# One transpose for the oldest and the own key tile, and one for the global keys of four units, in a sliding-window attention and FFN layer

## The reference, cut to what matters

```python
# attention of one sequence: T = 2048 tokens, D = 2048, 16 heads of 128, G = 16 global tokens
xn = layernorm(x) * ln_scale + ln_bias
xg = concat([global_tokens, xn])
Q, K, V = xg @ Wq.T, xg @ Wk.T, xg @ Wv.T
band = (j <= i) & (j >= i - 256 + 1)          # plus: every token sees the 16 global keys
attn = softmax(Q @ K.T / sqrt(128) masked by band)
x = layernorm(x + (attn @ V) @ Wo.T + x)
# ffn, hidden size 5632, weights as integers 0..255
x = layernorm(x + down(silu(gate(x)) * up(x)))
```

## Time and profile before

| what | value |
|---|---|
| time, median of 3 runs | 3033.59 us (3030.71 to 3200.52) |
| the profiled execution's own time | 3030.48 us |
| its span, slowest core (core 1) | 3028.9 us; all cores 3017.3 to 3028.9 us |
| mean granted TensorE clock of the cores | 0.993 to 0.995 |
| PE busy | 2943.5 us, 97% of the span, 16928 matmuls |
| PE weight loads busy | 1517.8 us, 50% |
| DVE busy | 1112.9 us, 37% |
| ACT busy | 603.1 us, 20% |
| POOL busy | 213.3 us, 7% |
| chain that ended last | PE 95%, DVE 1%, DMA 1%, ACT 1%, issue 1% |

### The profile page before, as it was taken

How to read it: one execution, slowest core, us unless ns; L and a number is a source line. 1 busy time by engine, 2 the same in 40 slices (tenths; PEclk the granted TensorE clock), 3 DMA queues, 4 the chain that set the end, 5 groups by cost and what they waited for, 6 DMA issues and landing times.

```text
span 3028.9 us, 43253 instructions; the slowest of 8 cores (3017.3 to 3028.9 us)
## 1 busy us (share of the span) xinstructions
PE 2943.5 (97%) x16928; PEld 1517.8 (50%) x16928; DVE 1112.9 (37%) x2185; ACT 603.1 (20%) x1364; POOL 213.3 (7%) x349
## 2 busy tenths in 40 slices
PE   4899999999999999999999999999999999999998
PEld 2566666666665444444444444444444444444443
DVE  5645555555556564112121211111222333212224
ACT  4434444444444111000000000000111111100000
POOL 0000000000000000000000000010000000012220
PEclk9999999999999999999999999999999999999999
DMA  7132413223214563434343435565655555448442
GB/s 200 69 57 46 74 33 68 52 41 64 54 25 150 170 205 112 84 70 84 70 83 70 82 65 104 104 109 143 132 115 122 113 123 126 97 103 189 77 77 112
DMA packets 93944, 293.54 MB, mean 97 GB/s; under 512 B 9008, under 2 KB 33840, under 8 KB 82480
## 3 DMA queue, kind: packets, MB, share of 16 engines
q0 software_dynamic: 46224, 172.05, 33.5%
q1 hardware_dynamic: 46656, 118.02, 11.1%
q10 hardware_dynamic: 864, 0.70, 0.1%
HBM read 412.45 MB, written 50.33 MB: 153 GB/s over the span
## 4 chain that ended last, share of the span: by engine, by line
PE 95%; DVE 1%; DMA 1%; ACT 1%; issue 1%; POOL 0%; DVEq 0%; ACTq 0%; SPq 0%; POOLq 0%
PE pb L789 40%; PE pb L836 19%; PE pb L341 14%; PE pb L372 7%; PE pb L725 7%; PE pb L453 2%; PE pb L472 2%; PE pb L419 1%; ACT xnfmt L313 1%; DMA wdt<-wd 1%; DVE smt L272 1%; PE pb L394 0%; PE pb L707 0%; PE pb L302 0%; DMA xt<-x 0%
## 5 line engine op out<-in xcount | busy, mean ns | idle before, releaser
L789 PE MATMUL pb<-xn2t,wgt 128*128 128x512 bf16 x2816 | 636.5, 379 | 0.0
L789 PE MATMUL pb<-xn2t,wut 128*128 128x512 bf16 x2816 | 636.5, 379 | 0.0
L341 PE MATMUL pb<-xnfmt,wqkt 128*128 128x512 bf16 x2048 | 537.2, 382 | 10.5 <-ACT kgt L364 5.8
L803 DVE SCALAR_TENSOR_TENSOR hmidt<-pb,sutt,silt 128x512 bf16<-128x512 f32 x176 | 132.2, 751 | 908.0 <-PE pb L789 898.3
L836 PE MATMUL pb<-wdt,hmidt 128*128 128x512 bf16 x2048 | 446.8, 380 | 7.3 <-DVE wdt L686 6.1
L789 PEld LDWEIGHTS pb<-xn2t,wut 128*128 128x128 bf16 x2816 | 275.5, 98 | 332.3
L789 PEld LDWEIGHTS pb<-xn2t,wgt 128*128 128x128 bf16 x2816 | 275.6, 98 | 331.9
L799 ACT ACTIVATE silt<-pb,sgtt 128x512 f32<-128x512 f32 x176 | 119.9, 687 | 1288.8 <-PE pb L789 1288.7
L836 PEld LDWEIGHTS pb<-wdt,hmidt 128*128 128x128 bf16 x2048 | 200.8, 98 | 251.5 <-issue 12.0
L372 PE MATMUL pb<-wvt,xnfmt 128*128 128x256 bf16 x2048 | 269.0, 273 | 0.0
L341 PEld LDWEIGHTS pb<-xnfmt,wqkt 128*128 128x128 bf16 x2048 | 173.8, 98 | 142.0 <-issue 20.7
(11 more groups left out here) (73 smaller groups left out, 1867.0 us busy)
## 6 DMA issues: line engine op xcount, KB each, us to landing
wgt<-wg POOLq DMA_DIRECT2D x88, 512.0 KB, 5.2
wut<-wu POOLq DMA_DIRECT2D x88, 512.0 KB, 7.2
wdt<-wd POOLq DMA_DIRECT2D x64, 512.0 KB, 5.9
xt<-x SPq DMA_DIRECT2D x16, 1024.0 KB, 8.9
v1t<-x SPq DMA_DIRECT2D x16, 1024.0 KB, 5.4
r2sp<-v1t SPq DMA_DIRECT2D x16, 1024.0 KB, 3.9
wdx<-wd POOLq DMA_DIRECT2D x24, 512.0 KB, 5.7
wqkt<-wk POOLq DMA_DIRECT2D x16, 512.0 KB, 8.2
```

What stands on the lines that cost most here:

```text
L341: t1 = op("pe", lambda e, dc=dc: e.matmul(pb[bank][:, :], w[:, dc * 128:(dc + 1) * 128], xnfm[:, dc * T + b * 512:dc * T + (b + 1) * 512], ...
L789: ins = e.matmul(pb[bank][:, :], w[gu][:, dc * 128:(dc + 1) * 128], xn2[p][:, dc * 1024 + tc * 512:dc * 1024 + tc * 512 + 512], start=(dc ...
L803: bfree[bu] = sil_free[s] = op("dve", lambda e, bu=bu, s=s, hsl=hsl: e.scalar_tensor_tensor(hsl, pb[bu][:, :], sut[:, hb:hb + 1], silt[s][ ...
```

## The change

The scores are computed as before. Then, for a unit with t of at least 2, the own tile's scores are overwritten with the oldest tile's wherever the mask allows the oldest tile (a predicated copy, L465 in the new file), which leaves 272 columns in place of 400 for the maximum, the exp and the scaling. The scaling writes t-1 and the merged tile (256 columns) to `pnt` and the 16 global columns to `pgt`, at columns 32*(u%4), which collects four units. PE transposes the merged tile and t-1 (2 in place of 4), and after every fourth unit's scaling `pgt`. A predicated copy (DVE, 256 columns, its source the merged tile read twice) splits the merged tile into the oldest and the own part of `ptt`, which was zeroed once; ACT then copies the rest (128 columns, or 256 with the global tile), after the DVE copy. P times V has three matmuls for a unit; the four global ones follow after the fourth unit, each with a `vgt` of its own that has the 16 global rows at partitions 32*u. To make these, `proj_vg` computes V of the global tokens transposed (32 matmuls of 16 moving columns), ACT writes it four times to `zgt` (4 copies of 2x16 columns), and `turn_vg` transposes it (2) and copies it out four times (ACT, 16 partitions x 256). `proj_vg` moves to the front of its block and `turn_vg` stands before the Q/K projections. A mask of 64 KB is loaded by one more DMA on ACT's queue, and more tiles are zeroed at the start.

```diff
-    for b in pn + vg:
+    t_msplit = dma("act", s_c[4], msplit[:, :], ms_in[:, :])
+    for b in pg + pt + vg[0] + vg[1] + [zg]:
         t_zero = op("dve", lambda e, b=b: e.memset(b[:, :], 0.0))
...
     def proj_vg(j):
+
         bank = pj_bank()
 
         def f(e):
-            for dc in range(ND):
-                ins = e.matmul(pb[bank][0:G, 0:256], g_fm[:, dc * G:(dc + 1) * G],
-                               wvt[:, dc * 256:(dc + 1) * 256], start=(dc == 0), stop=(dc == ND - 1))
+            for i in range(2):
+                for dc in range(ND):
+                    ins = e.matmul(pb[bank][:, i * G:(i + 1) * G],
+                                   wvt[:, dc * 256 + i * 128:dc * 256 + (i + 1) * 128],
+                                   g_fm[:, dc * G:(dc + 1) * G], start=(dc == 0), stop=(dc == ND - 1))
             return ins
         t1 = op("pe", f, t_wv[j], t_g, bfree.get(bank))
         t_wvfree[j] = t1
-        bfree[bank] = t_vg[j] = op("dve", lambda e: e.tensor_copy(vg[j % 2][0:G, :], pb[bank][0:G, 0:256]),
-                                   t1, t_zero, t_pv.get((2 * j - 3, NT - 1)))
-        yield 16
+        z = zg[:, :].rearrange("p (i u k) -> p i u k", i=2, u=4)
+        for u in range(4):
+            t2 = op("act", lambda e, u=u: e.copy(
+                z[:, :, u, 0:G], pb[bank][:, 0:2 * G].rearrange("p (i k) -> p i k", i=2)),
+                t1, t_zero, t_vg.get(j - 1))
+        bfree[bank] = t_vgz[j] = t2
+        yield 4
+
+    def turn_vg(j):
+
+        n = nstep[0] - 2
+        bank = 7 if n < 16 else 7 - 2 * (n // 4 % 2)
+        dst = pb[bank][:, :].bitcast(BF16)
+
+        def f(e):
+            for i in range(2):
+                ins = e.transpose(dst[:, i * 128:(i + 1) * 128], zg[:, i * 128:(i + 1) * 128],
+                                  ident[:, :])
+            return ins
+        t1 = op("pe", f, t_vgz[j], bfree.get(bank))
+        for u in range(4):
+            t2 = op("act", lambda e, u=u: e.copy(
+                vg[j % 2][u][32 * u:32 * u + G, :], dst[32 * u:32 * u + G, 0:256]),
+                t1, t_zero, t_pv.get((2 * j - 3, NT - 1)))
+        bfree[bank] = t_vg[j] = t2
+        yield 1
...
-        if lo == 0:
-            edge = pb[bank][:, :].rearrange("p (a k) -> p a k", a=2)[:, :, 0:128]
-            mk = mask[:, :].rearrange("p (a k) -> p a k", a=2)
+
+        own = pb[bank][:, 256:384]
+        if t >= 2:
+            t2 = op("dve", lambda e: e.copy_predicated(
+                own, mask[:, 0:128].bitcast(I32), pb[bank][:, 0:128]), t1, t_mask)
         else:
-            edge = pb[bank][:, 256:384]
-            mk = mask[:, 128:256]
-        t2 = op("dve", lambda e: e.tensor_tensor(edge, edge, mk, ALU.add), t1, t_mask)
+            t2 = op("dve", lambda e: e.tensor_tensor(own, own, mask[:, 128:256], ALU.add),
+                    t1, t_mask)
...
+        op("dve", lambda e: e.tensor_scalar(
+            pn[u % 3][:, lo - 128:256], s[:, lo:384], r[:, 2:3], None, ALU.mult),
+            t1, t_t.get(u - 3))
         t_p[u] = op("dve", lambda e: e.tensor_scalar(
-            pn[u % 3][:, lo:SW], s[:, lo:SW], r[:, 2:3], None, ALU.mult), t1, t_zero, t_t.get(u - 3))
+            pg[u // 4 % 2][:, 32 * (u % 4):32 * (u % 4) + G], s[:, 384:SW], r[:, 2:3], None,
+            ALU.mult), t_zero, t_t.get(u // 4 * 4 - 5))
...
-            for j in range(lo // 128, 4):
-                ins = e.transpose(trb[k][:, j * 128:(j + 1) * 128],
-                                  pn[u % 3][:, j * 128:(j + 1) * 128], ident[:, :])
+            ins = e.transpose(trb[k][:, 0:128], pn[u % 3][:, 128:256], ident[:, :])
+            if t > 0:
+                ins = e.transpose(trb[k][:, 128:256], pn[u % 3][:, 0:128], ident[:, :])
+            if end == 384:
+                ins = e.transpose(trb[k][:, 256:384], pg[u // 4 % 2][:, :], ident[:, :])
             return ins
+        free = t_pv.get(units[u - 3]) if u >= 3 else None
         t_t[u] = op("pe", f, t_p[u], bfree.get(k))
-        bfree[k] = t_pt[u] = op("act", lambda e: e.copy(pt[u % 3][:, lo:512], trb[k][:, lo:512]),
-                     t_t[u], t_pv.get(units[u - 3]) if u >= 3 else None)
+        t1 = op("dve", lambda e: e.copy_predicated(
+            p[:, 0:256].rearrange("p (a k) -> p a k", a=2),
+            msplit[:, :].rearrange("p (a k) -> p a k", a=2).bitcast(I16),
+            trb[k][:, 0:128].unsqueeze(1).broadcast_to([128, 2, 128])), t_t[u], free, t_msplit, t_zero)
+        if t > 0:
+            t1 = op("act", lambda e: e.copy(p[:, 256:end + 128], trb[k][:, 128:end]), t1, free)
+        bfree[k] = t_pt[u] = t1
...
+            if t % 4 == 3:
+                for i in range(4):
+                    ins = e.matmul(pb[k][:, i * 128:(i + 1) * 128], vg[j % 2][i][:, o:o + 128],
+                                   p[:, 384:512], start=False, stop=(i == 3))
...
-    run(proj_vg(0), vt(0, range(0, 2), "act"), transposed([4, 5], AD))
+    run(proj_vg(0), vt(0, range(0, 2), "act"), turn_vg(0), transposed([4, 5], AD))
...
-                gens.append(proj_vg(j + 1))
+                gens = [proj_vg(j + 1)] + gens[:-1] + [turn_vg(j + 1)] + gens[-1:]
```

More of the change, by code:

```diff
@@ L179, in build_nc @@
     A1 = TP
-    pn = [at("pnt%d" % i, 512, BF16, A1 + 1024 * i) for i in range(3)]
+    pn = [at("pnt%d" % i, 256, BF16, A1 + 512 * i) for i in range(3)]
+    pg = [at("pgt%d" % i, 128, BF16, A1 + 1536 + 256 * i) for i in range(2)]
+    zg = at("zgt", 256, BF16, A1 + 2048)
+    msplit = at("msplitt", 256, BF16, A1 + 2560)
     aostg = [at("aostg%d" % i, 512, BF16, A1 + 3072 + 1024 * i) for i in range(2)]
-    vg = [at("vgt%d" % i, 256, BF16, A1 + 5120 + 512 * i) for i in range(2)]
+    vg = [[at("vgt%d" % (4 * i + k), 256, BF16, A1 + 8192 + 512 * (4 * i + k)) for k in range(4)]
+          for i in range(2)]
     kg = [at("kgt%d" % i, G, BF16, A1 + 6144 + 64 * i) for i in range(2)]
@@ L411, in lo_of @@
     def lo_of(t):
-        return max(2 - t, 0) * 128
+        return 256 if t == 0 else 128
     def u_scores(u):
@@ L416, in u_scores @@
         lo, par, bank = lo_of(t), h % 2, 2 + u % 2
+        s0 = max(2 - t, 0) * 128
         def f(e):
-            e.matmul(pb[bank][:, lo:384], qb[par][:, t * 128:(t + 1) * 128],
-                     kb[par][:, (t - 2) * 128 + lo:(t + 1) * 128], start=True, stop=True)
+            e.matmul(pb[bank][:, s0:384], qb[par][:, t * 128:(t + 1) * 128],
+                     kb[par][:, (t - 2) * 128 + s0:(t + 1) * 128], start=True, stop=True)
             return e.matmul(pb[bank][:, 384:SW], qb[par][:, t * 128:(t + 1) * 128], kg[par][:, :],
```

32 lines of the change are left out of this document (19 added, 13 removed).

## The result

The changed kernel takes **3009.3 us** (median of seven runs). The ratio to the kernel before, measured beside it, is 0.9921 with a 95% interval of 0.9901 to 0.9940. The same source run again a while later gave 3007.8 us and 0.9913 (0.9881 to 0.9944). Three of the seven executions were slowed by a lower granted clock on one die or both, so the ratios use undisturbed executions alone, which took 3004.8 to 3009.3 us here; where disturbed ones would spoil a median further down, only the ratio is given. The forecast was 3009 us in a range of 2998 to 3023: the time lies inside, and that it meets the median to 0.3 us is luck, as the median is the upper end of that span. But the interval stands clear of 1: this is a gain of 0.8% that the runs do tell from no change, and the prediction had called it "within 2%", with a chance of 96%.

A forecast was written before the change was run, and what follows sets the result against it. PE was taken as the attention stage's bound: -28.8 us on PE, +2.9 at the start, +3 at head starts and +0.6 at the end give -22.3 us, hence 3009 us, range 2998 to 3023.

The forecast's parts named there:

- The bound: Attention stage: PE busy 248.4 of 250 us, so almost every matmul start removed shortens it if other queues keep up.
- The transposes: Attention units on PE: 416 fewer transposes at 55 ns each, -22.9 us; `turn_vg` adds 16, +0.9 us.
- the weight load's 90 ns: Rival for PE's transposes: each removed one gains its weight load's time, 90 ns, not 55; 2994 us, chance 3%.
- The global V projection: PE, eight times: 32 matmuls of 16 moving columns take 1.0 us in place of 1.85, -6.8 us.
- (a) The start: Until about 150 us: `vgt` copies ahead of `xnfmt` and extra DVE work delay PE, +2.9 us, ends +1.5 and +5.
- (b) Head starts: Even heads from 4 on: K projection waits for the last Q projection's bank, +3 us in all, ends 0 and +8.
- (c) The end: Last head's `aostg` copy to first output projection: less PE work beside two DMAs, the 1.9 us wait grows +0.6.
- DVE costs nothing in the ordinary steps: Attention units: 318 ns more DVE work each, DVE 166 of 250 us (66%), hidden below PE.
- both upper ends: Predicated copies at their highest assumed costs, 575 and 692 ns: DVE 207 of 250 us, still below PE.
- DVE deciding only from 1.8 us: Rival, attention units: DVE becomes the bound if both predicated copies exceed 1.8 us, not 0.73; 3121 us at 2.2, chance 3%.
- if a predicated copy is over 0.9 us: Sign in DVE's attention work that the forecast is wrong: one predicated copy above 0.9 us, where 299 and 432 ns were taken.
- half of it is lost in new waits: Rival: the PE-DVE-ACT-PE path of `ptt` holds up PE, 0.05 us in 240 units, +12 us, 3021 us; chance 13%.

The follow-up runs named there:

- the half gain of the global keys: Changed kernel without merging and splitting of tiles: only the global keys of four units collected, with the new global V projection; stage 889.2 us, ratio 0.9981.

## Why the prediction was right, and where it was wrong

**The step that failed** is the sentence "A measurement of this kernel can tell about 2% (61 us) from no change, so this counts as within 2%". The runs tell far less from no change: one kernel measured twice gave 0.9921 and 0.9913, with intervals of 0.2 and 0.3% to either side, and the half gain of the global keys, 0.9981, still has an interval (0.9969 to 0.9992) that leaves 1 out. A forecast of -22 us with a range ending at 3023 us, 10 us below the median, was itself a forecast of "faster", and the chance should have stood there. The threshold was taken over and not read from the runs. They were at hand: three of the kernel before, two of them within 3 us. Two steps of the mechanism were wrong as well, though the time did not show it: the waits at head starts, and DVE's room.

**The bound (right).** PE's starts decide; the transposes put back took most of the gain away again, 18.8 of 24.4 us.

**The transposes (right).** Forecast 55 ns each, measured 56. The chance of 3% for the weight load's 90 ns was not too small. The Trainium skill ("TensorE: Matmul & The Clock Gate", Back-to-back issue gap) says 81 ns for a stream with weight loads; this case's trace has a load for every transpose and 56 ns between starts, and does not agree.

**The global V projection (right).** Forecast 1.0 us in place of 1.85. Timeline of PE in the changed kernel:

```profile
290.78 0.95 PE L405 MATMUL pb<-g_fmt,wvt 128*128 128x16 bf16 x32
292.13 1.03 PE L379 MATMUL pb<-wvt,xnfmt 128*128 128x256 bf16 x8 [0.40 <-ACT zgt L413]
```

292.13 - 290.78 - 0.40 of waiting = 0.95 us, 30 ns a matmul.

**(a) The start (+2.9 forecast, near).** The piece ahead of head 2 has 21 transposes fewer, with those of `turn_vg(0)`, and a projection shorter by 0.85 us: 2.0 us. It came out 0.3 us longer, so 2.3 us are lost, inside the ends of 1.5 and 5. That the four `vgt` copies ahead of `xnfmt` are part of it is shown by moving them (-2.5).

**(b) Head starts (+3 forecast, mis-sized).** On the mean of eight cores, from 190 to 938 us, the wait for `kgt` went from 4.9 to 6.7 us, and new are `zgt` 2.3, `qbt` 0.4 and `aostg` 0.2: +4.6. (The slowest cores alone, whose rows stand further up, give +5.6.) The forecast had the even heads' wait for the bank, with 0.4 us each:

```profile
304.63 0.55 PE L367 MATMUL pb<-g_fmt,wqkt 128*128 128x16 bf16 x16
305.63 0.59 PE L348 MATMUL pb<-xnfmt,wqkt 128*128 128x512 bf16 x2 [0.45 <-ACT kgt L371]
```

That one is 0.45. What it lacked is the second wait in the same block, behind the global V projection (0.40 in the rows further up). The new projection is too short to cover the copy of the bank that the next one needs, exactly as the K one is in the earlier trace rows; that reading was at hand and was applied once.

**(c) The end (+0.6 forecast).** In the slowest cores the wait for `aobt` is 2.7 us and was 1.9. But on the mean of eight cores the piece from head 15 on is 1.5 us shorter, and its 26 transposes fewer are worth 1.5 to 1.7: at most 0.2 us are lost.

**Sum.** The starts of PE inside the stage, mean of eight cores, with idle times over 0.05 us counted as waits:

| | forecast us | measured us |
|---|---|---|
| transposes, net | -22.0 | -22.2 |
| global V projection | -6.8 | -7.0 |
| waits of PE, (a) to (c) | +6.5 | +5.1 |
| V projection matmuls | 0 | -0.8 |
| the rest | 0 | +0.5 |
| stage | -22.3 | -24.4 |

Between heads 2 and 15 the waits are 4.0 us longer, where 3 were forecast, and the V matmuls win back 1.6 that nobody forecast, as PE waits less for their copies; the start and the end lose about 1 us less than forecast. (Of the 2.3 us of (a), 0.9 stand in the table under waits, 0.9 under V projection matmuls and 0.5 in the rest.) So a loss set too low met a gain not seen, and that the sum is only 2.1 us off is in part luck.

**"DVE costs nothing in the ordinary steps" (right in the sum, wrong in its reason).** At these prices PE indeed has no listed wait for `ptt` behind 186 us. But the room was read from the busy share: at both upper ends "83%: still below PE", and DVE deciding only from 1.8 us for both predicated copies together. DVE stops at 80% of busy time, since each of its instructions in the chain waits for one before it. By that text one more split copy (1.1 us for the three, by busy time) costs nothing, and it cost 22 us. With 0.95 us for the split (two copies, start of the first to end of the second) only 2.4 of the 24.4 us are left. This much the prediction had given as a sign of being wrong ("if a predicated copy is over 0.9 us"). Its upper end of 692 ns lies between the two and was not run, so whether 13% for "half of it is lost in new waits" was too small stays open.

## What to carry over

Cost an instruction that joins a chain across engines by what waits in order behind its receiver, not by the busy share of its own engine: here 0.5 us per unit cost 22 us inside the chain and 4 beside it. When a projection is made shorter or moved, look at which copy it covered, and give short projections a bank that is free already. And take what a measurement can tell from the spread of its runs before saying that a forecast of 0.7% is no change.
